# Head sums divided and projected inside the score steps instead of after them, and a token-major last stage

## The reference

```python
    # narrow attention (cross-attention of the last layer; the others lack gate and nan_to_num)
    scores = jnp.einsum('bhqd,bhkd->bhqk', q, k) / jnp.sqrt(jnp.float32(dk))
    attn = jax.nn.softmax(masked(scores), axis=-1)
    context = jnp.einsum('bhqk,bhkd->bhqd', attn, v)
    output = gate * context @ Wo.T            # gate = sigmoid(query @ Wg.T + bg)
...
    # last feed-forward
    h = x
    for blk in range(3):
        y = _qlora_linear(h, qweights[2*blk], ...)       # x @ dequant(q).T + bias + (x @ la.T) @ lb.T
        y = gelu(_layernorm(y, ln_gamma[blk], ln_beta[blk]), approximate=False)
        h = _qlora_linear(y, qweights[2*blk+1], ...) + h
    return h
```

## Time and profile before

| | us |
|---|---|
| median of 3 runs (range) | 1764.23 (1762.51 to 1765.19) |
| profiled execution, its time | 1759.35 |
| profiled execution, its span | 1757.6 |
| PE busy | 1491.2, 85% of the span |
| DVE busy | 1012.8, 58% |
| ACT busy | 797.9, 45% |
| POOL busy | 449.6, 26% |
| mean granted TensorE clock | 0.917 |

### The profile page before, as it was taken

The page is one execution under the profiler, slowest core; times in us unless marked ns, Lnnn a source line. Parts: engine busy times, 40 slices in busy tenths (PEclk is TensorE's granted clock), DMA queues, the critical chain, the costliest instruction groups (busy, mean ns, idle before and its releaser), DMA issues. The chain is left out here.

```text
span 1757.6 us, 30799 instructions
## 1 busy us (share of the span) xinstructions
PE 1491.2 (85%) x10804; PEld 754.0 (43%) x10823; DVE 1012.8 (58%) x1950; ACT 797.9 (45%) x1407; POOL 449.6 (26%) x652
## 2 busy tenths in 40 slices
PE   7998999999659999579767899989648888788798
PEld 5777534444424445247433532222305333433266
DVE  5665598883452222546547478994564674467234
ACT  3554447677223333116330237778243564366334
POOL 6121300000234442410235220000023452255200
PEclk9999999999979999689887899999858899999888
DMA  2000542120200000001000163120002421431000
GB/s 94 1 0 0 152 160 84 41 54 1 116 0 0 1 0 0 0 19 36 5 6 1 59 195 121 50 53 15 14 0 83 152 65 29 149 95 54 15 1 24
DMA packets 82104, 85.63 MB, mean 49 GB/s; under 512 B 7085, under 2 KB 67757, under 8 KB 81613
## 3 DMA queue, kind: packets, MB, share of 16 engines
q1 hardware_dynamic: 82008, 84.40, 15.3%
HBM read 51.28 MB, written 32.51 MB: 48 GB/s over the span
## 5 line engine op out<-in xcount | busy, mean ns | idle before, releaser
L1282 ACT ACTIVATE arena<-ps 128x1024 f32<-128x1024 f32 x256 | 262.1, 1024 | 111.9 <-PE ps L1191 111.1
L1176 PE MATMUL ps<-k_stack,q_stack 49*128 49x512 bf16 x512 | 192.5, 387 | 15.2 <-DVE small L1306 13.0
L1191 PE MATMUL ps<-q_stack,k_stack 51*128 51x256 bf16 x1024 | 191.6, 275 | 0.5 <-ACT arena L1282 0.4
L1303 DVE CUSTOM_DVE_ANT_0 small<-ps,mask_b 128x512 bf16<-128x512 f32 x256 | 168.1, 689 | 33.7 <-PE ps L1176 32.1
L1306 DVE TENSOR_REDUCE small<-ps 128x1 f32<-128x512 f32 x256 | 162.2, 685 | 22.5 <-PE ps L1176 21.4
L1492 DVE TENSOR_REDUCE small<-ps 128x6 f32<-128x768 f32 x128 | 122.6, 958 | 76.3 <-PE ps L1374 74.6
L1203 PE MATMUL ps<-arena,v_pad 128*32 128x256 f32 x2048 | 163.7, 394 | 1.1 <-ACT arena L1282 1.1
L1468 ACT ACTIVATE arena<-ps 128x384 f32<-128x384 f32 x256 | 117.8, 488 | 72.9 <-PE ps L1393 72.0
L1076 POOL TENSOR_SCALAR_AFFINE_SELECT arena<-arena 128x256 f32<-128x256 f32 x256 | 102.3, 408 | 80.7 <-ACT arena L1468 80.4
L2543 DVE TENSOR_TENSOR arena<-ps,arena 128x512 f32<-128x512 f32 x64 | 44.3, 692 | 120.9 <-PE ps L2509 120.9
L2558 POOL TENSOR_TENSOR arena<-arena 128x512 f32<-128x512 f32 x64 | 81.1, 1267 | 108.8 <-DVE arena L2543 107.0
(11 more groups left out here) (343 smaller groups left out, 3061.6 us busy)
## 6 DMA issues: line engine op xcount, KB each, us to landing
q_stack<-q_scratch SPq DMA_DIRECT2D x128, 96.0 KB
k_stack<-k_scratch SPq DMA_DIRECT2D x64, 192.0 KB
k_scratch<-arena SPq DMA_DIRECT2D x8, 768.0 KB, 3.7
k_stack<-k_scratch SPq DMA_DIRECT2D x64, 96.0 KB
q_scratch<-arena SPq DMA_DIRECT2D x4, 1152.0 KB, 5.5
arena<-in_ctxT SPq DMA_DIRECT2D x8, 512.0 KB, 6.8
k_scratch<-arena SPq DMA_DIRECT2D x8, 512.0 KB, 4.7
k_scratch<-arena SPq DMA_DIRECT2D x16, 256.0 KB, 4.5
```

Of the source, the lines that this page charges most:

```text
L1176: pe.matmul(ps[:, t, :], c.q_stack[par][64 * e:64 * e + ROW_MAX, pr, t * P:(t + 1) * P], c.k_stack[par][64 * e:64 * e + ROW_MAX, pr, :], s ...
L1191: mm = pe.matmul(ps[:, bank, (ch % 2) * S:(ch % 2 + 1) * S], c.k_stack[prv][64 * e:64 * e + ROWS, pr, ch * P:(ch + 1) * P], c.q_stack[prv] ...
L1282: act.activation(buf.probs[i % 8], ps[:, bank:bank + 2, :].rearrange("p a n -> p (a n)"), ACT.Exp, scale=scale).then_inc(g["probs"].sem, 1)
L1303: dve.tensor_tensor_reduce(buf.junk[t], ps[:, t, :], c.mask_b[:, M_X + t * SC:M_X + (t + 1) * SC], 1.0, FLOOR, op0=ALU.add, op1=ALU.max, a ...
```

## The change

1. `combine` is gone. A new class `Outputs` does its work for one batch at a time. In step s, SP stores the sums of batch s-2 to DRAM (`store_sums`, 4 DMAs from 9 partitions each), loads them back as a 128-row tile (8 rows times 16 heads) and the denominators as 128 by 32 (`load_sums`, 2 DMAs); DVE inverts that small tile; SP stores the inverses to DRAM, waits until they have landed, and loads them 8 times, once for each 16 rows (`spread_inverse`, 1 + 8 DMAs). In the next step the quotient is made (POOL in `attend_wide`, DVE in `attend_short`), in w_l3x multiplied by the gate on POOL, projected on PE at i = 7 into bank 7, and added to x (ACT copy and POOL add in `attend_wide`, one DVE operation in `attend_short`). For the last batch the denominators are loaded spread at once and inverted as 128 by 256.
2. The gate's sigmoid moves to the end of `project`.
3. `lora_ffn` is one block (between the first norm products PE does the LoRA centring, weights 0 and 1 and `up` of tiles 0 and 1): POOL dequantises while the norm runs, the weights are built between the norm's products, mean subtraction is folded into the up weights, `up` gives tokens in rows, so that ACT sums squares per token, DVE scales, PE transposes back, ACT does the gelu. POOL makes the last sum of x and h early.

```diff
-    combine(c, slot, **how)
@@ attend_transfers, one step
             load(s, 1)
         if s:
             place(s - 1, 1)
+        if s > 1:
+            outs.store_sums(buf, sp, s - 2)
         if s in (1, 2):
             store_parts(c, sp, "k", nk, s + 1, s + 2, g[f"stored_k{s + 1}"].sem)
         if 1 <= s < B - 1:
             load(s + 1, 0)
+        if s > 1:
+            outs.load_sums(sp, s - 2)
         if s < B:
             place(s, 0)
+        if s > 1:
+            outs.spread_inverse(sp, s - 2)
+    outs.store_sums(buf, sp, B - 1)
+    outs.load_sums(sp, B - 1, True)
@@ class Outputs
+    def store_sums(self, buf, sp, b):
+        for i in range(2):
+            sp.wait_ge(g[f"summed_out{i}"].sem, g[f"summed_out{i}"].at(2 * b + 2))
+        for j in range(4):
+            sp.dma_start(c.sum_scratch[b, :, GROUPS * j:GROUPS * j + GROUPS, :],
+                         buf.summed[32 * j:32 * j + DH + 1, :, b * S:(b + 1) * S]).then_inc(g["sums_stored"].sem, 16)
+    def spread(self, sp, out, src, sem):
+        for d in range(DH):
+            sp.dma_start(out[H * d:H * d + H, :], src).then_inc(sem, 16)
+    def load_sums(self, sp, b, last=False):
+        sp.wait_ge(g["sums_stored"].sem, g["sums_stored"].at(64 * (b + 1)))
+        if b > 1:
+            sp.wait_ge(g["quotient"].sem, g["quotient"].at(b - 1))
+        sp.dma_start(self.num[b % 2], c.sum_scratch[b, 0:DH, :, :].rearrange("d q n -> (d q) n")).then_inc(sem, 16)
+        if last:
+            self.spread(sp, self.rec[b % 2], c.sum_scratch[b, DH, :, :], sem)
+        else:
+            sp.dma_start(self.den[b % 2], c.sum_scratch[b, DH, :, :].rearrange("q (a n) -> (q a) n", a=P // H)).then_inc(sem, 16)
+    def spread_inverse(self, sp, b):
+        sp.wait_ge(g["inverted"].sem, g["inverted"].at(b + 1))
+        sp.dma_start(c.inv_scratch[b, :, :].rearrange("q (a n) -> (q a) n", a=P // H), self.den[b % 2]).then_inc(g["inv_stored"].sem, 16)
+        sp.wait_ge(g["inv_stored"].sem, g["inv_stored"].at(16 * (b + 1)))
+        self.spread(sp, self.rec[b % 2], c.inv_scratch[b, :, :], g[f"inv_spread{b % 2}"].sem)
+    def divide(self, eng, par, half, done="quotient"):
+        eng.wait_ge(g[f"inv_spread{par}"].sem, g[f"inv_spread{par}"].at(16 * DH * half + 16 * DH))
+        eng.tensor_tensor(self.quot[par], self.num[par], self.rec[par], ALU.mult).then_inc(g[done].sem, 1)
@@ attend_short, DVE, one step of 8 pairs
+                    if late and pr == 2:
+                        outs.divide(dve, 1 - par, it - 2 + par)
+                    if late and pr == 3:
+                        outs.add(dve, s - 3, 7)
+                    if before and pr == 5:
+                        outs.invert(dve, par, it - 1, s - 2)
@@ lora_ffn, PE (new)
+            norm_pe(norm, pe, follow=follow)
+            for blk in range(NB):
+                for t in TS:
+                    if blk or t >= 2:
+                        up(blk, t)
+                if blk == 0:
+                    weights(2, NL, 6)
+                    keep_clock(c, pe, 8, bank=7)
+                for t in TS:
+                    for ch in range(4):
+                        mm = pe.transpose(ps[:, 4 + t, ch * P:(ch + 1) * P], chunk(z, t, ch), c.ident[:, :])
+                    if t:
+                        pe.matmul(ps[:, t - 1, :], wT[:, 2 * blk + 1, :], act_out[:, t - 1, :], start=True, stop=True)
@@ lora_ffn, ACT (new), one block
+                for t in TS:
+                    for ch in range(4):
+                        mm = act.activation(chunk(act_out, t, ch), chunk(y, t, ch), ACT.Square, accum_out=ssq[:, 4 * t + ch:4 * t + ch + 1])
+                act.activation(dev, ssq, ACT.Sqrt, bias=c.consts[:, C_EPS:C_EPS + 1], scale=1.0 / D)
```

More of the change, by code:

```diff
@@ L885, in _ @@
             second(len(units) - 1)
+            if gated:
+                for t in TS:
+                    act.wait_ge(g["gate_in"].sem, g["gate_in"].at(t + 1))
+                    act.activation(norm.tile(c.xn, t), ps[:, 2 + t % 2, :], ACT.Sigmoid, bias=w[:, W_BG:W_BG + 1])\
+                       .then_inc(g["gate_out"].sem, 1)
         @block.vector
@@ L1058, in attend_pool, with step @@
     pool.wait_ge(g["cleared"].sem, g["cleared"].at(1))
-    def step(it, par, front, back, before):
+    def step(it, par, front, back, before, late):
         s = it * 2 + par
@@ L1063, in step @@
             attend_split(c, buf, pool, s - 1, 1, 1 - par)
+        if late and not causal:
+            outs.divide(pool, 1 - par, it - 2 + par)
         for i in range(H):
@@ L1076, in step @@
                 pool.affine_select(diag, diag, [[0, 2], [1, P]], ALU.is_ge, 0.0, 0, -1).then_inc(g["masked"].sem, 1)
+            if late and outs.gated and i == 4:
+                outs.gate(pool, 1 - par, s - 3)
             if front and i == (9 if causal else 0):
                 attend_split(c, buf, pool, s, 0, par)
+        if late and not causal:
+            pool.wait_ge(g["out_kept"].sem, g["out_kept"].at(s - 2))
+            xb = c.xT[:, bass.ds((s - 3) * S, S)]
+            pool.tensor_tensor(xb, xb, outs.kept[1 - par], ALU.add).then_inc(g["residual"].sem, 1)
     attend_steps(c.nc, ENG.Pool, step, causal)
+    if outs.gated:
+        for b in (B - 2, B - 1):
+            outs.gate(pool, b % 2, b)
 def turned_max(c, hf):
@@ L1139, in sum_waits, with project_late, attend_wide @@
         pe.wait_ge(out.sem, out.at(b * 2 + grp // 2))
+    if grp == 1 and late:
+        pe.wait_ge(g[emptied].sem, g[emptied].at(b - 1))
     if grp == 0 or grp == 2 and front:
         pe.wait_ge(g["turned_out"].sem, g["turned_out"].at(b * 2 + 2 + grp // 2))
-def attend_wide(c, masked):
+def project_late(c, outs, pe, s, par):
+    out = c.sig["summed_out1"]
+    pe.wait_ge(out.sem, out.at((s - 1) * 2))
+    outs.project(pe, 1 - par, s - 3, 7)
+def attend_wide(c, masked, slot, guard=False, gated=False):
     nc, g, ps = c.nc, c.sig, c.ps
     buf = AttendBuffers(c, True)
+    outs = Outputs(c, slot, c.xn[:, :], guard, gated)
     nch = SC // P
@@ L2897, in lora_ffn @@
-    g.advance(weights_in=64, made=2, turned=2)
-    with nc.Block() as block:
-        @block.tensor
-        def _(pe):
-            def spread(n, t):
-                pe.wait_ge(g["ln_rstd"].sem, g["ln_rstd"].at(n + t + 1))
-                norm_spread(c, pe, rstd[:, 4 * t:4 * t + 4], ps[:, 4 + t, :]).then_inc(g["ln_spread"].sem, 1)
-            for blk in range(3):
+            dve.tensor_tensor(centring, c.ident[:, :], c.mean_w[:, :], ALU.subtract).then_inc(g["centring"].sem, 1)
+            norm_dve(norm, dve)
```

491 lines of the change are left out of this document (260 added, 231 removed).

## The result

The changed kernel takes 1808.94 us (median of 4 runs, 1803.85 to 1813.53), the kernel before 1763.37 in the runs beside it (1759.31 to 1765.19): a ratio of 1.0262, 95% interval 1.0229 to 1.0295. It is slower by some 46 us, where 40 were forecast.

The account below looks back on a forecast made before the run. SP's in-order queue was taken to set the short steps, PE or DVE the wide ones. Short steps +56.6, tails -7.5, wide steps and gate +4.4, last stage -14: +39.5, so 1798.9 profiled, 1804 as median; range 1758 to 1832.

Parts of the forecast that it names:

- Short steps: w_l3a and w_l3x: SP's in-order queue lengthens the 12.9 us steps; +22.2 and +34.4 us, together +56.6.
- Wide steps: w_l0x and w_l2x: SP's chain stays hidden; PE's projection costs 2.2 us, DVE's small inversion 1.2.
- Hidden, with 1.4 us of room: Wide steps: second place comes 9.9 us after the first, within a half period of 11.3 or 12.85.
- up to 5 if it must wait for the landing: w_l2x: upper bound on the 1.2 us term for DVE's small inversion.
- Tails: Last-batch work replacing the four combines: 13.6 us ungated, 14.6 with guard and gate; together -7.5 us.
- The 4.6 us of lateness: End of both short attentions: SP's chain for batch 6 makes the tail start 4.6 us late.
- Gate: Gate's PE and ACT work moved to the end of `project`, beside SP's loads: 1 us, bounds 0 to 5.
- Last stage: New `lora_ffn`: earlier `up` and shorter blocks, -20 us in the working, -14 taken for the clock; bounds -22 and 0.
- A: Rival: added DMAs are hidden in the short steps too, program ends faster at 1738 us; chance 0.15.
- B: Rival: issue pitch holds but landings are quick or slack larger; short steps +28, time 1775; chance 0.12.
- C: Rival: PE pauses in short steps and may fall to 1.2 GHz; +20, time 1824; chance 0.25 with D.
- D: Rival: the last stage gains 0 instead of -14, time 1818; chance 0.25 together with C.

Follow-up runs that it names:

- the transfers alone: Changed kernel, short attentions keeping all DMAs, small inversion and SP's waits, but without division, gate product, projection and add for batches 0 to 5: 1810.20 us, ratio 1.0312.
- the kernel with the arithmetic alone: Changed kernel, short attentions keeping inversion, division, gate, projection and add, but without stores, loads and spreads for batches 0 to 6: 1769.36 us, ratio 1.0056.

## Why the prediction was right

**Short steps.** Forecast +22.2 and +34.4, measured +22.7 and +32.7. That the transfers in SP's order are the cause is shown from three sides: they alone bring the whole loss, taking them out brings back 35 us, and issuing alone, with nothing behind it, brings 3.7 and 12.9 in the kernel before. How they cost it was only in part as forecast. "Each microsecond by which SP is late is one that PE stands still" does not hold: of the 51.0 us more between the first and last merged rows PE stands for 15.8 and is busy for 35.2, of which some 27 (estimate, as above) are the lower clock. The sum had the clock, together with slower landings, at about half a us a step, 5 in all. That the totals agree to 2 us is therefore partly luck.

The parts of the chain in w_l3a, steps 3 to 6: first place to second place 9.9 forecast, 8.4 to 10.1 measured; second to first 6.4 forecast, 6.2 to 8.1 measured; and step 2, for which about 1 us more was forecast, is 6.8 longer than before. Inside the first part, in the step shown, two errors cancel: the inverse is ready 3.2 us after the place's start instead of 2.1 (the denominators are used 3.6 us after their issue), and its store lands in 1.4 instead of 2.2. In w_l3x the parts are 10.3 to 11.0 and 6.7 to 8.2, forecast 11.4 and 7.2; there the queue goes from its loads to the place without a pause in nine of the twelve half-steps from step 2 on, so that it is late throughout. One expected sign is nearly missing: from step 2 on PE's waits for the place itself came to only 0.4 us in w_l3a and 2.7 in w_l3x (6.9 and 10.3 with the transfers alone). PE stands behind DVE and in many short pauses instead. DVE's wait in front of the denominators was not in the forecast, and what share of the loss goes through it cannot be told, since moving it moves the loss. Nor can the share of the clock: a slower PE also delays the maxima and the inversion for which SP waits, and no run separates the two.

**Wide steps: the failed step.** "Hidden, with 1.4 us of room" was right for the second place, but the forecast looked at places only. The bound named for w_l2x, "up to 5 if it must wait for the landing", was the case that occurred, in w_l0x as well: 8.1 and 6.8 us of it, taken out by one moved inversion. With the projection at 0.70 instead of 0.45 and the inversion at 0.35 instead of 0.2 the term was +26.3 instead of 3.4, its largest error.

**Tails.** -17.0 instead of -7.5. A tail takes 12.7 us in w_l0x, 13.6 forecast, and `combine` of w_l3a, which the forecast took at 15.1, had 16.7. The 4.6 us of lateness in the short ones came to 1.5 and 3.1 (14.2 against 12.7, and 16.8 against 13.7 with guard and gate): the store of the last sums starts at once behind the spreads of batch 6 (1520.62 to 1520.72), and part of the lateness lies in the last step (+3.5 in w_l3a, forecast 1.7).

**Gate.** +5.0 from w_l3a's last add to w_l3x's first merged row, forecast 1. The kernel with only the gate moved has 2.9, inside the bounds of 0 to 5; the rest goes with a granted clock of 0.90 instead of 0.96 over this stretch, after an attention in which PE paused. That this is the reason is not shown; the kernel with the last stage alone has 40.3 there at 0.92, without the gate. The cost in the first step behind it (19.2 us against 18.0) was in no term.

**Last stage.** The working gave -20, the forecast took -14 for fear of the clock; measured -19.4. Squares to squares the blocks take 14.9 and 16.6 us, forecast 17.1, from these windows of the changed kernel:

```profile
1760.74:1775.60 14.86, 14.26 (x83) 9.95 (x83) 9.25 (x25) 11.66 (x42) 0.00 (x0) 1.00 0.00 0
1775.60:1792.21 16.61, 12.13 (x59) 8.23 (x58) 9.25 (x25) 11.18 (x42) 4.47 (x4) 0.79 0.01 1
1792.21:1808.17 15.96, 10.70 (x42) 6.30 (x40) 8.55 (x24) 9.69 (x39) 0.59 (x1) 0.79 0.11 40
```

The feared clock came, 0.79 in the last two blocks, and the second block is 1.7 us longer than the first, which had 1.00. But 16 squares take 4.8 us at a pitch of 0.30 instead of 5.6, and the last block takes 16.0 from its squares to its last add. The start gained less than forecast: the first squares run 24.3 us into the stage, where the working put them at 19.9 (`up` at 1682, 18.2 after the last add of 1663.80, and 1.7 for its first tile and y).

**The rivals.** A (all hidden) is out: a spread costs 0.45 us to issue. The rule of the Trainium skill weighed in the forecast (DMA: Bandwidth & Descriptors, Issuing engines are not separate DMA queues), that a sequencer's time to initiate a DMA is usually small beside the DMA, holds for the single store of inverses (0.33 us of issuing, landed 1.4 after its start) but does not make the sum of the queue small: the issuing of eight loads alone cost 12.9 us in w_l3x. B (+28 in short steps) is out by their size. C, the clock, is real and larger than its price in the sum: 0.81 and 0.77 over the two short attentions where it was 0.95, and 2.4 us of PE's time in a step of the kernel with the arithmetic alone, where the pauses were waits for POOL. The Trainium skill's section HAM oscillation (TensorE: Matmul & The Clock Gate) describes a kernel that is throttled again at each wait for a DMA, and the runs agree in kind. It does not come on top of the queue's loss, as C had it (the steps are no longer than forecast); it is inside it. Where the queue is late anyway a slow PE may cost nothing of its own; in the step of 19.1 us at 0.50 it set the length. How much of the 51 us would be left at full clock is open. D is out; the last stage gained more than forecast.

**The total.** The terms were 39.5; the two spans differ by 53.3. The 13.8 between them are, measured less forecast, +22.9 (wide steps), +4.0 (gate), +3.0 (stretches that the change does not touch), -1.2 (short steps), -9.5 (tails) and -5.4 (last stage). So 29.9 us that the terms lacked stand against 16.1 that they had too much; that the total came out as near as it did is in part luck. The forecast is nearer still to the median, 1804 to 1809, because the profiled execution after lies 3.6 above its median, where the one before lay below.

## What to carry to other kernels

Before work is moved into a loop, look at the tightest loop it enters and there at the issuing queue in its own order: each DMA of these sizes costs it 0.3 to 0.65 us, and each store, load and compute round trip that it waits out stands ahead of the transfers that the engines need. Ask the same of every compute engine that gets a new wait: name what is queued behind it, and take the landing time behind the largest stores, not the median. And run the parts of a large change alone: here the last stage, one of the three parts, made the program 1.5% faster alone, and the head sums inside the steps brought nearly all the loss. And read PE's busy time and granted clock beside its waits: pauses of about 1 us, none of which looked like much, went with a clock that made the same products take longer.

## What the runs showed of the hardware

- One DMA whose source is repeated eight times took 0.65 us of SP's time; eight DMAs for the same rows took 3.57.
- The load of the denominators, 16 KB, was used 3.6 us after its issue in the step of w_l3a shown, and 4.4 us after it behind three k stores of w_l0x, though DVE stood ready both times; the forecast had 2.0.
- Two pauses of PE of about 1 us, 3 us apart, were followed by a stretch of some 6 us in which the same products took 0.61 instead of 0.39 us. In another kernel the granted clock stayed at 0.50 over a step of 19.1 us in which PE was busy for 18.9.
- Eight unused loads of 16 KB a step in SP's queue, with nothing added to any other engine, went with a granted clock over w_l3x of 0.85 instead of 0.95 and a busy time of PE of 91.7 us instead of 82.7 for the same instructions.
- The stretch before the first attention, the same work in every kernel here, took 228.6 to 235.5 us from one execution to the next; the execution with 235.2 had a granted clock of 0.83 in its first 50 us, the one with 230.8 had 0.93. A difference of 5 us between two single profiles says nothing by itself.
- ACT's square of 128 columns with its sum per row has a pitch of 0.30 us; the reading of the accumulator, 0.19, lies beside the next square's start:

```profile
1761.05 0.29 ACT L3062 ACTIVATE arena<-arena 128x128 f32<-128x128 f32 x1
...
1761.25 0.19 ACT L3062 ACTIVATION_READ_ACCUMULATOR arena<-arena 128x1 f32 x1
1761.34 0.29 ACT L3062 ACTIVATE arena<-arena 128x128 f32<-128x128 f32 x1
```
